# A gated recurrence with a mixture of experts behind it: where TensorE's side work stands in a step, and how the start is arranged

## What is computed

```python
# stage 1: four experts and a shared one, all run on every token
for e in range(4):
    h = gelu(x @ ew1[e] + eb1[e])                  # 256 -> 1024
    out += w_be[:, e] * mask[e] * (h @ ew2[e] + eb2[e])   # 1024 -> 256
x = x + out + gelu(x @ sw1 + sb1) @ sw2 + sb2
# w_be: softmax gate over 4 experts, the best 2 kept, one weight per sequence and expert
# stage 2: GRU, one step per token, h is 2 x 256
z = sigmoid(x_t @ W_z + h @ U_z + vz)
r = sigmoid(x_t @ W_r + h @ U_r + vr)
hh = tanh(x_t @ W + (r * h) @ U + vh)
h = (1 - z) * h + z * hh
x_t = x_t + h
```

## Time and profile before

| what | value |
|---|---|
| time, median of 3 runs | 1961.99 us (1953.92 to 1963.96) |
| the profiled execution's own time | 1969.93 us |
| its span, first to last instruction | 1968.1 us |
| TensorE busy, weight loads busy | 1937.5 us (98%), 1749.9 us (89%) |
| VectorE, ScalarE, GpSimd busy | 1188.3, 689.9, 216.7 us |
| mean granted TensorE clock | 0.978 |
| first product of step 0 | 65.96 us |

### The profile page before, as it was taken

One profiled execution on the slowest core, in us unless ns is written; L12 is line 12 of the kernel. 1 busy time (PEld: TensorE's weight loads), 2 busy tenths in 40 slices (PEclk: granted clock), 3 DMA queues, 4 the chain that ended last, 5 costly groups with the idle time before them and its releaser, 6 DMA issues.

```text
span 1968.1 us, 102687 instructions
## 1 busy us (share of the span) xinstructions
PE 1937.5 (98%) x42900; PEld 1749.9 (89%) x42978; DVE 1188.3 (60%) x8413; ACT 689.9 (35%) x3780; POOL 216.7 (11%) x520
## 2 busy tenths in 40 slices
PE   8899999999999999999999999999999999999998
PEld 7898998989899898998989989898998989989765
DVE  5465665656556565665656666565665656656555
ACT  3233333333333333333333333333333333333222
POOL 2310101101011010101101011010100101011000
PEclk8999999999999999999999999999998999999999
DMA  8000000000000000000000000000000000000000
GB/s 306 2 5 5 4 5 5 4 5 5 4 5 4 4 5 4 5 5 4 5 4 4 5 5 4 5 5 4 5 5 4 5 5 4 5 5 4 5 5 4
DMA packets 16911, 23.69 MB, mean 12 GB/s; under 512 B 3585, under 2 KB 15160, under 8 KB 16445
## 3 DMA queue, kind: packets, MB, share of 16 engines
q1 hardware_dynamic: 15280, 17.05, 2.5%
q10 hardware_dynamic: 1164, 0.07, 0.0%
HBM read 15.01 MB, written 2.10 MB: 9 GB/s over the span
## 4 chain that ended last, share of the span: by engine, by line
PE 96%; POOL 1%; issue 1%; DVE 1%; ACT 1%; ACTq 0%; DVEq 0%
PE r_ps L783 19%; PE up_ps L689 19%; PE y_ps L707 19%; PE c_ps L783 16%; PE z_ps L783 16%; PE up_ps L818 4%; PE c_ps L723 1%; PE r_ps L723 1%; PE z_ps L723 1%; PE z_tanh_ps L729 1%; PE y_ps L718 1%; POOL uf L339 0%; POOL uf L341 0%; ACT hidden L397 0%; POOL wx L349 0%
## 5 line engine op out<-in xcount | busy, mean ns | idle before, releaser
L689 PE MATMUL up_ps<-feat,up_w 128*128 128x128 f32 x2528 | 526.3, 307 | 3.7 <-ACT hidden L397 3.7
L707 PE MATMUL y_ps<-hidden,down_w 128*128 128x128 f32 x2528 | 526.9, 306 | 0.0
L611 DVE TENSOR_TENSOR_SCAN h_cur<-rc_tanh_ps,blend 128x8 f32<-128x8 f32 x1024 | 177.8, 174 | 379.4 <-ACT rc_tanh_ps L403 378.0
L783 PEld LDWEIGHTS r_ps<-h_cur,u_high 128*128 128x128 f16 x4096 | 251.8, 96 | 148.2 <-DVE h_cur L611 69.2
L403 ACT ACTIVATE rc_tanh_ps<-r_ps 128x4 f32<-128x4 f32 x1024 | 161.8, 158 | 624.9 <-PE r_ps L783 624.9
L689 PEld LDWEIGHTS up_ps<-feat,up_w 128*128 128x128 f32 x2528 | 371.0, 195 | 8.4 <-ACT hidden L397 7.9
L707 PEld LDWEIGHTS y_ps<-hidden,down_w 128*128 128x128 f32 x2528 | 368.5, 194 | 2.3
L783 PE MATMUL r_ps<-h_cur,u_high 128*128 128x20 bf16 (+5 forms) x4096 | 350.9, 180 | 1.5 <-DVE h_cur L611 0.3
L783 PE MATMUL c_ps<-p_cur,u_high 128*128 128x40 bf16 (+10 forms) x4096 | 345.1, 181 | 2.2
L595 DVE SCALAR_TENSOR_TENSOR p_cur<-rc_tanh_ps,h_cur 128x4 f32<-128x4 f32 x1024 | 166.9, 163 | 294.9 <-ACT rc_tanh_ps L403 291.9
L783 PE MATMUL c_ps<-p_cur,u_mid 128*128 128x40 bf16 (+10 forms) x4096 | 339.7, 180 | 0.0
(11 more groups left out here) (137 smaller groups left out, 2963.0 us busy)
## 6 DMA issues: line engine op xcount, KB each, us to landing
up_w<-in_L_cond_ew SPq DMA_DIRECT2D x4, 1024.0 KB, 9.1
down_w<-in_L_cond_ew SPq DMA_DIRECT2D x4, 1024.0 KB, 11.9
x_rows<-in_x SPq DMA_DIRECT2D x8, 256.0 KB, 4.9
out<-out_rows SPq DMA_DIRECT2D x128, 16.0 KB, 1.8
up_w<-in_L_cond_sw SPq DMA_DIRECT2D x1, 1024.0 KB, 13.3
down_w<-in_L_cond_sw SPq DMA_DIRECT2D x1, 1024.0 KB, 13.9
cf<-in_L_cond_C_r SPq DMA_DIRECT2D x1, 256.0 KB, 5.7
cf<-in_L_cond_C_z SPq DMA_DIRECT2D x1, 256.0 KB, 5.9
```

What stands on the lines that cost most here:

```text
L611: dve.tensor_tensor_scan(h_cur[:, 0, :], cand, blend[:, :], 0.0, ALU.mult, ALU.add).then_inc(part_ready, 1)
L689: last = mm(up_ps[n % 2][:, 0:COLS], up_w[:, e, k, j * P:(j + 1) * P], feat[:, k, c * COLS:(c + 1) * COLS], start=(k == 0), stop=(k == KC ...
L707: last = mm(y_ps[:, m * COLS:(m + 1) * COLS], down_w[:, e, j, m * P:(m + 1) * P], hidden[:, n % TILES_HELD, :], start=False, stop=(m == KC ...
L783: return mm(gate_ps[g][:, at:at + width], w[:, g, k, m * P:(m + 1) * P], moving, start=False, stop=last_of_sum, skip_group_check=True)
```

## The change

Three things are changed.

In the step, `side(c, t, 0)` moves from behind gate z's products to between gate r's and gate z's. What it holds stays the same.

At the front of a chunk, one filler product (`IDLE`, in the bank of the tile under way, columns 128 on) is put between the two halves of each of the first three up products. The list of side work so grows from 162 pieces to 165 a chunk. The filler of window 1 shrinks from 512 to 384 columns, and all fillers now accumulate into columns 128 on.

In the prologue, the splitting of U goes from GpSimd to VectorE, gate by gate in three operations over 512 columns, with the scaling of tiles in between; the largest entry of U is taken directly after the gate's weights are spread. The scaling of W goes from GpSimd to ScalarE, between gelus 24, 26 and 28. The gate's exponential goes behind gelu 3. The condition's products and the gate's logits go between the first up products.

```diff
-IDLE_FILL = (256, 512)
+IDLE_FILL = (256, 384)
+IDLE_AT = 128
...
-            units += [(UP, i, 0), (UP, i, 1)]
+            units += [(UP, i, 0), *([(IDLE, i, 0)] if i < LAG else []), (UP, i, 1)]
...
-            pool.wait_ge(w_scale_made, 1)
-            flat = lambda w: w[:, :, :, :].rearrange("p g k n -> p (g k n)")
-            pool.tensor_scalar(flat(uf), flat(uf), w_scale[:, :], FP16_MAX, ALU.mult, ALU.min).then_inc(u_chain, 1)
...
-            for g in range(GATES):
-                w = wx[:, g, :, :].rearrange("p k n -> p (k n)")
-                pool.tensor_scalar(w, w, gain(g), None, ALU.mult).then_inc(wx_scaled, 1)
...
-            act.wait_ge(logits_shifted, 1)
-            act.activation(score[:, :], logit[:, :], ACT.Exp).then_inc(exp_made, 1)
...
             for i in range(len(TILES[0])):
                 gelu(0, i)
+                if i == 3:
+                    act.wait_ge(logits_shifted, 1)
+                    act.activation(score[:, :], logit[:, :], ACT.Exp).then_inc(exp_made, 1)
+                if i in (24, 26, 28):
+                    g = (i - 24) // 2
+                    act.wait_ge(wx_in, 16 * GATES)
+                    w = wx[:, g, :, :].rearrange("p k n -> p (k n)")
+                    act.activation(w, w, ACT.Copy, scale=gain(g)).then_inc(wx_scaled, 1)
...
+            for g in range(GATES):
+                dve.tensor_scalar(mats(uf, g), mats(uf, g), w_scale[:, :], FP16_MAX, ALU.mult, ALU.min
+                                  ).then_inc(u_chain, 1)
+                scale_first(10 + 4 * g, 11 + 4 * g)
+                dve.wait_ge(u_chain, 2 * g + 1)
+                dve.tensor_scalar(mats(u_high, g), mats(uf, g), -FP16_MAX, None, ALU.max).then_inc(u_chain, 1)
+                scale_first(11 + 4 * g, 12 + 4 * g)
+                dve.wait_ge(u_chain, 2 * g + 2)
+                dve.scalar_tensor_tensor(mats(u_mid, g), mats(uf, g), -FP16_MAX, mats(u_high, g), ALU.max,
+                                         ALU.subtract).then_inc(u_split, 1)
+                scale_first(12 + 4 * g, 14 + 4 * g)
...
+                if i == 1:
+                    pe.wait_ge(cond_mats_in, 16 * GATES)
+                    cond_part(R)
+                if i == 2:
+                    pe.wait_ge(agg_made, 1)
...
+                    cond_part(Z)
+                if i == 3:
+                    cond_part(C).then_inc(gbias_summed, 1)
...
-            pe.wait_ge(u_split, 1)
+            pe.wait_ge(u_split, GATES)
...
+            def idle(window, bank=0):
+                mm(up_ps[bank][:, IDLE_AT:IDLE_AT + IDLE_FILL[window]], ident16[:, :], keep_warm[:, 0:IDLE_FILL[window]],
+                   start=False, stop=True, skip_group_check=True)
+
...
+                    elif what == IDLE:
+                        if c < CH - 1:
+
+                            idle(window, (TILE0[c + 1] + of[0]) % 2)
...
                 last.then_inc(preact, 1)
+                side(c, t, 0)
                 for product in HIGH_PRODUCTS:
                     recur(s, Z, False, product)
                 for product in LOW_PRODUCTS:
                     last = recur(s, Z, True, product, product is LOW_PRODUCTS[-1])
                 last.then_inc(preact, 1)
-                side(c, t, 0)
                 pe.wait_ge(part_ready, parts + PARTS_STEP + P_HIGH)
```

More of the change, by code:

```diff
@@ L80, in moe_gru_kernel @@
             SCALED[TILE0[c] + i] = n_scaled
-    UP, DOWN, BIAS, TURN, PROJECT = "up", "down", "bias", "turn", "project"
+    UP, DOWN, BIAS, TURN, PROJECT, IDLE = "up", "down", "bias", "turn", "project", "idle"
     SIDE = {(t, w): [] for t in range(CT) for w in range(2)}
@@ L505, in _ @@
                               ).then_inc(spread_made, 1)
+            dve.wait_ge(u_in_sem, 16 * GATES)
+            link(dve.tensor_reduce(umax[:, :], uf[:, :, :, :].rearrange("p g k n -> p (g k n)"), AX.X,
+                                   ALU.max, apply_absolute_value=True))
+            dve.tensor_scalar(umax[:, :], umax[:, :], 2.0 ** -100, None, ALU.max).then_inc(umax_local, 1)
             dve.wait_ge(weights_shared, 1)
@@ L526, in scale_first @@
                         scale_tile(dve, 0, i, e, scaled_first)
[L528 to L534, removed]
+            scale_first(0, 6)
             dve.wait_ge(gbias_summed, 1)
@@ L541, in _ @@
                               ).then_inc(gbias_made, 1)
+            scale_first(6, 10)
             dve.wait_ge(umax_shared, 1)
@@ L546, in _ @@
             link(dve.tensor_scalar(w_scale[:, :], w_scale[:, :], 2.0 ** 14, GAIN * 2.0 ** -6, ALU.mult, ALU.min))
-            dve.tensor_scalar(w_scale[:, :], w_scale[:, :], GAIN * 2.0 ** -14, None, ALU.max).then_inc(w_scale_made, 1)
-            dve.wait_ge(w_scale_made, 1)
+            link(dve.tensor_scalar(w_scale[:, :], w_scale[:, :], GAIN * 2.0 ** -14, None, ALU.max))
             link(dve.reciprocal(half_s[:, 0:1], w_scale[:, :]))
@@ L551, in _ @@
             dve.tensor_copy(half_s[:, 1:ST], half_s[:, 0:1].broadcast_to([P, ST - 1]))
-            link(dve.tensor_scalar(h_unscale[:, :], w_scale[:, :], 1.0 / GAIN, None, ALU.mult))
-            scale_first(8, 12)
+            dve.tensor_scalar(h_unscale[:, :], w_scale[:, :], 1.0 / GAIN, None, ALU.mult)
             def seed(c, g, m):
@@ L558, in seed, with mats @@
                                 gate_bias[:, g, m, :].unsqueeze(1).broadcast_to([P, CT, B])).then_inc(seeded, 1)
+            def mats(w, g):
+                return w[:, g, :, :].rearrange("p k n -> p (k n)")
+            for g in range(GATES):
[9 more added lines that the diff above has]
+                scale_first(12 + 4 * g, 14 + 4 * g)
             dve.wait_ge(gbias_made, 1)
@@ L564, in _ @@
                     seed(0, g, m)
-                    scale_first(12 + 2 * (g * KC + m), 14 + 2 * (g * KC + m))
+                    scale_first(22 + g * KC + m, 23 + g * KC + m)
             dve.memset(cand, 0.0)
+            scale_first(28, len(TILES[0]))
             make_rows(CT, T).then_inc(rows_made, 1)
-            scale_first(24, len(TILES[0]))
             def residual(c, k):
@@ L657, in _ @@
                skip_group_check=True)
-            pe.wait_ge(cond_mats_in, 16 * GATES)
             cond_v = small_cols[:, ROW_COND:ROW_COND + B * KC].rearrange("p (b k) -> p k b", k=KC)
@@ L668, in cond_part @@
                 return last
[L670 to L679, removed]
             def up(c, i, k):
@@ L736, in _ @@
                         up(0, i, k)
+                if i == 1:
[3 more added lines that the diff above has]
+                    pe.wait_ge(agg_made, 1)
+                    for q in range(3):
+                        for k in range(KC):
+                            mm(y_ps[0:B, 64 + 2 * E:64 + 3 * E], agg[:, q, k, :], gate_w_sb[:, q, k, :], start=False,
+                               stop=False, skip_group_check=True)
+                    mm(y_ps[0:B, 64 + 2 * E:64 + 3 * E], ones[0:1, 0:B], bias_row[:, 2 * E:3 * E], start=False,
+                       stop=True, skip_group_check=True).then_inc(logits_made, 1)
+                    cond_part(Z)
+                if i == 3:
+                    cond_part(C).then_inc(gbias_summed, 1)
                 if i == FIRST_LAG:
@@ L817, in side @@
                     for _ in range(1 + window - turning):
-                        mm(up_ps[0][:, 0:IDLE_FILL[window]], ident16[:, :], keep_warm[:, 0:IDLE_FILL[window]],
-                           start=True, stop=True, skip_group_check=True)
+                        idle(window)
             for s in range(T):
```

7 lines of the change are left out of this document (removed).

## The result

The changed kernel takes 1980.58 us (median of 4 runs, 1979.51 to 1982.47) against 1961.44 for the one before (4 runs beside it): ratio over the runs 1.0113, 95% interval 1.0089 to 1.0136 (the two medians alone give 1.0098). By the medians it is slower by 19 us, where the forecast was 10. The profiled execution took 1979.51, 9.6 more than the profiled one of before at 1969.93.

What follows compares the result with a forecast made beforehand. TensorE looks 98% busy, but the step is a chain where it waits for VectorE. Terms -7.5 - 5.7 + 31.5 + 3.5 + 1.5 - 13 = +10.3, put on the median 1962, gave 1972 us, range 1936 to 1988.

Steps and rivals of the forecast that it cites:

- I put the difference on the median: Last step of the sum: profiled execution is 8 above the median by falls, so 1962 + 10 = 1972.
- Falls of the clock, -13: Behind chunk fronts: four or five falls left instead of eleven, 9.5 us of 22.5; between -22 and 0.
- z's chain, +31.5: In the step: side work ahead of z delays the scan by 0.035 us, 60 steps in 15 chunks.
- The rival in which z keeps its slack: In the step: z's first product follows the piece sooner, scan goes by the candidate; 1935.5 us, chance 0.19.
- The front, -5.7: Front of a chunk: fillers keep two gelus from holding one step to 2.20 instead of 1.82, 0.38 x 15.
- The prologue, -7.5: Prologue: projection no longer waits for W and runs at full clock, -8.5, against +1 for the condition's products.
- the +1 for the condition's products: Prologue: the condition's products enter the run of tiles and cost +1 us, between -1 and +4.
- Pauses and seeds: In the step: 13 VectorE pauses without slack, +3.5 us; copies that seed a gate bank, +1.5, between 0 and 5.
- The last chunk's shorter filler, "at nothing": Last chunk: the shorter filler costs nothing, its clock being 1.00 and its window having a wait of 0.6 us.
- fell as often as before: Rival on the chunk fronts: bias steps alone cause the falls, +13 comes back; 1985 us, chance 0.18.
- stopped falling: Rival on the chunk fronts: no fall of the clock is left; 1962.5 us, no change, chance 0.14.
- the prologue kept its gain: Answers the rival that first tiles running longer at the low clock use up the 8.5; 1979.5 us, chance 0.05.

Runs made afterwards that it cites:

- e8: The kernel before with the five rows of the bias products padded by zeros to 128, nothing else; 1940.79 us, ratio 0.9873.
- e10: The kernel before with the new prologue and padded bias products, no pacing, side work behind z; 1934.12 us, ratio 0.9843.
- e4: The kernel before with fillers in the front and shorter fillers elsewhere, nothing else; 1951.94 us, ratio 0.9940.
- e2: The changed kernel with the side work put back behind z's products; 1946.48 us, ratio 0.9911.
- e1: The kernel before with only the side work of window 0 moved in front of z's products; 1997.33 us, ratio 1.0160.
- e9: The changed kernel with side work behind z, padded bias products, two 256-column fillers per front filler, 512 in pieceless windows; 1929.12 us, ratio 0.9816.
- e6: The changed kernel with VectorE's two waits ahead of the scan exchanged, blends first; 2040.99 us, ratio 1.0384.

## Why the forecast was half the size

The direction was right, and so was the mechanism of the largest term; the total against the profiled execution was 1980, which is what the changed kernel takes. **The step that failed is the last one of the sum, "I put the difference on the median", with the falls of the clock left at -13.** That the sum fits the profiled execution so closely is in part luck: a cost of 10 us was missing from it, and two terms were off the other way.

*The carry-over.* Over 31 runs of the kernel before, time rises with the time at 1.2 GHz (twice the span times one minus the mean clock) by 0.31 us per us, from 1942 at none. The median run of these, clock 0.982, has 71 us of it and so loses 22; the profiled one, 0.978, has 87 and loses 27. These 5 us are most of what lies between the profile and the 31 runs' median, 1963.9; the four runs beside the changed kernel have a median 2.5 lower, and their clocks are not on record. Against the 31 runs the changed kernel is 17 us slower. The forecast saw that the profile was 8 above the median by falls of the clock, then credited 13 for falls that the change removes, and subtracted the 8 as well. But a change that takes falls away can't win back those that the median run doesn't have. By the forecast's own figures the median run has 22.5 - 8 = 14.5 us of falls; with 9.5 left, the term for it is -5 and not -13, and the sum is +18, near what was measured. The changed kernel's runs lie within 3 us of each other, clock 0.989 to 0.991, whatever the profile of before had. The sum on the profiled execution, 1980, should have stood.

*Falls of the clock, -13.* In the profiles the loop's time beyond its common steps, falls and VectorE's pauses together, went from 23.3 to 8.1: -15.2, where the forecast had -13 + 3.5 = -9.5. The 22.5 that it counted for the falls before was right: the steps with a fall in chunks 1 to 14 are together 22.2 longer than the same steps at 2.4 GHz. Its reason was half right at most: with the five-row products padded no fall is left although the step is still held (e8, e10), and with the fronts paced they become fewer but stay (e4, e2). Why the moved side work leaves fewer falls with the five-row products still there is not settled; e1 has fewer in its loop than before as well (44 us at 1.2 GHz against 68).

*z's chain, +31.5.* The chain is as forecast, instruction by instruction: 0.33 from the piece's load to z's first product, scan 0.26 behind the blend. The size is 0.031 a step, not 0.035: 47 ordinary steps x 15 x 0.031 = 22, about 26 over all steps with a piece. The rival in which z keeps its slack is out. The Trainium skill, page "TensorE: Matmul & The Clock Gate", section "Step-by-step: what each phase is for", has weight loads pulled ahead of products in flight. The trace agrees: z's load at 207.81 lies under the piece's loads, which last to 207.89. It bought nothing, for the product still starts at 207.92, 0.33 behind the piece's load.

*What was not forecast.* The late second blend holds the transposes of the turning steps, 8.9 us in the 45 steps 18, 34 and 50 (of which 1.4 are the ordinary growth), leaves step 2 at 1.96 (15 x 0.11 = 1.6), and holds the projection's products into z's bank, so that step 61 takes 1.91 (0.9). I followed what waits for the scan and not who else waits for the blends. These 10 us were covered in the sum by the z term, 5 too large, and by the falls, about 5 too small; that is luck.

*The front, -5.7.* e4 and e2 give it exactly, 1.82. In the changed kernel, with z late, step 2 falls from 2.20 to 1.96 only, which is -3.6.

*The prologue, -7.5.* Right in the profile: 67.60 to 60.13; over all profiles the gain lies between 4.8 and 8.0. The later features (54.13 to 55.33) are the +1 for the condition's products.

*Pauses and seeds.* About ten of VectorE's pauses now show, 0.35 each, against +3.5. The copies that seed a bank, +1.5, cost nothing: their steps are 0.005 longer and the steps behind them 0.005 shorter.

*The last chunk's shorter filler, "at nothing".* Its clock was wrong: 14.6 us at 1.2 GHz there instead of 0.6. In time it was nearly right, since those steps have slack: the chunk is 0.5 us longer in the changed kernel. With 512 columns (e9) the falls are gone.

*The rivals.* The clock neither fell as often as before nor stopped falling, the prologue kept its gain, and z has no slack: none of the four took the forecast's place, although two of their times (1985 and 1979.5) lie nearer to the result than 1972.

Profile against profile: -7.5 + 31.5 (the loop's common steps, forecast 27.3) - 15.2 + 0.7 (the last chunk and the end) = +9.5, measured 9.6.

## What to carry to other kernels

If a term of a sum is something that varies between runs, size it on the same run that the sum is added to. Either leave the whole sum on the profiled execution, or ask first how much of that term the median run has at all. When a value comes later, ask for every reader of the buffers it frees, not only for the next instruction on the critical chain; here a transpose four times a chunk cost about a third of what the delay of all steps cost. And look for the cheapest cause of a weak stretch first: zeros in 123 rows gave 23 us (e8), prologue and pacing together 17 (e2).

## What the runs showed of the hardware

- A float32 product with five rows lasts as long as one with 128 (L718: 319 ns in the kernel before; the padded ones 315), but the next work starts 0.41 after its load instead of 0.21. The Trainium skill, page "TensorE: Matmul & The Clock Gate", section "Why this matters for your kernels", says that a single product with 32 rows takes the same time as one with 128. That agrees with the instruction here (319 and 315 ns), though not with what follows it (0.41 and 0.21).
- With those rows padded the granted clock stayed at 2.4 GHz in chunks 0 to 14 of e8's profile, and its runs lie within 2 us; those of the kernel before lie within 20.
- Of two waits ahead of one VectorE instruction, the second costs 0.07 more than the first if it is the last to come (the scan 0.25 and 0.18 behind the start of the tanh, e6 and the changed kernel).
